# Two-layer transformer block on one core: second attention layer, weighted sums of the diagonal key tiles over all 512 queries

## The reference

```python
x = x + _L0_attn_ref(xn, ...) + _L0_ffn_ref(xn, ...)
xn = _layernorm(x, axis=-1)
x = x + _L1_attn_ref(xn, ...) + _L1_ffn_ref(xn, ...)
```

```python
scores = jnp.einsum('bhtd,bhsd->bhts', q, k)
mask = jnp.where(causal, 0.0, -jnp.inf)
probs = jax.nn.softmax((scores + mask) / jnp.sqrt(jnp.float32(dh)), axis=-1)
out = jnp.einsum('bhts,bhsd->bhtd', probs, v)
```

## Time and profile before

| | us |
|---|---|
| median of 3 runs | 2028.43 |
| lowest and highest of them | 2022.0, 2038.33 |
| the profiled execution | 2043.86 |
| its span, first to last instruction | 2042.1 |
| mean granted TensorE clock, share of full speed | 0.887 |

### The profile page before, as it was taken

The page is one execution under the profiler, slowest core; times in us unless marked ns, Lnnn a source line. Parts: engine busy times, 40 slices in busy tenths (PEclk is TensorE's granted clock), DMA queues, the critical chain, the costliest instruction groups (busy, mean ns, idle before and its releaser), DMA issues. The chain is left out here.

```text
span 2042.1 us, 35995 instructions
## 1 busy us (share of the span) xinstructions
PE 1633.4 (80%) x13931; PEld 819.6 (40%) x13931; DVE 1223.0 (60%) x2150; ACT 886.8 (43%) x1438; POOL 764.7 (37%) x423
## 2 busy tenths in 40 slices
PE   2468459879889898898989998345998889888887
PEld 2246325435354353544535443224654323333232
DVE  5323357686766757576576661481266877777761
ACT  0112215536456463564635455012322655555566
POOL 1500553564656656465564768260000111400000
PEclk9879759989899998999989999567998977888888
DMA  4113210000000000000000000123320000000000
GB/s 156 52 32 107 48 24 12 7 12 22 7 19 11 18 17 7 24 12 12 17 7 20 12 12 12 65 79 94 93 74 27 13 13 28 9 18 2 2 7 17
DMA packets 57109, 62.00 MB, mean 30 GB/s; under 512 B 12890, under 2 KB 42862, under 8 KB 56046
## 3 DMA queue, kind: packets, MB, share of 16 engines
q1 hardware_dynamic: 52846, 51.32, 8.1%
q0 software_dynamic: 4096, 8.40, 1.6%
HBM read 40.34 MB, written 18.48 MB: 29 GB/s over the span
## 5 line engine op out<-in xcount | busy, mean ns | idle before, releaser
L1582 POOL TENSOR_TENSOR a_prob_sum<-a_prob_sum,a_prob 128x1024 f32<-128x1024 f32 (+2 forms) x224 | 499.9, 2232 | 239.1 <-ACT a_prob L1530 218.2
L1530 ACT ACTIVATE a_prob<-a_st,a_table 128x512 f32<-128x512 f32 (+3 forms) x640 | 352.7, 626 | 358.3 <-PE a_st L1408 219.5
L1628 DVE TENSOR_REDUCE a_maxima<-a_ring 128x16 f32<-128x512 f32 (+3 forms) x640 | 352.8, 600 | 127.2 <-PE a_ring L1340 102.5
L1914 DVE TENSOR_REDUCE a_maxima<-a_mx 128x1 f32<-128x512 f32 (+3 forms) x640 | 352.3, 605 | 122.1 <-PE a_mx L1898 59.7
L2158 ACT ACTIVATE a_prob<-a_st 128x1024 f32<-128x1024 f32 (+3 forms) x320 | 269.0, 894 | 183.3 <-PE a_st L2076 102.4
L1435 PE MATMUL a_ot<-a_prob,a_values 128*64 128x512 f32 (+3 forms) x1280 | 289.0, 570 | 0.0
L1340 PE MATMUL a_ring<-a_k_hi,a_q_hi 64*128 64x512 f16 (+3 forms) x640 | 166.1, 373 | 94.2 <-DVE a_maxima L1628 71.6
L1898 PE MATMUL a_mx<-a_ks,a_qs 32*128 32x512 f16 (+3 forms) x640 | 188.3, 393 | 39.9 <-DVE a_maxima L1914 36.7
L2092 PE MATMUL a_ot<-a_prob,values_all 128*32 128x512 f32 (+3 forms) x1280 | 179.8, 638 | 0.2 <-ACT a_sums L2150 0.2
L2041 POOL DMA_INDIRECT a_back<-expert_out,slot_from x32 | 30.3, 948 | 347.7 <-ACT a_prob L2158 347.7
L1898 PEld LDWEIGHTS a_mx<-a_ks,a_qs 32*128 32x128 f16 x640 | 46.4, 93 | 246.8 <-DVE a_maxima L1914 173.8
(11 more groups left out here) (260 smaller groups left out, 2600.2 us busy)
## 6 DMA issues: line engine op xcount, KB each, us to landing
a_rden<-rden_wide SPq DMA_DIRECT2D x64, 128.0 KB, 2.9
f_w<-in_w SPq DMA_DIRECT2D x28, 256.0 KB, 2.8
expert_in<-zeros SPq DMA_DIRECT2D x5, 1024.0 KB, 11.2
f_rows<-expert_in SPq DMA_DIRECT2D x16, 256.0 KB, 3.7
expert_out<-f_result SPq DMA_DIRECT2D x16, 256.0 KB, 2.2
shared_w<-in_w SPq DMA_DIRECT2D x12, 256.0 KB, 3.1
a_table<-in_head_table SPq DMA_DIRECT2D x16, 140.5 KB, 2.2
parts<-part_t SPq DMA_DIRECT2D x4, 512.0 KB
```

The source lines that it names most:

```text
L1530: e = act.activation(prob[:, s % NPROB, a, c0:QW], ps_st[s % 2][:, a, c0:QW], ACT.Exp, bias=table[x][:, a, at:at + 1])
L1582: pool.tensor_tensor(into[:, :, c0:QW], into[:, :, c0:QW], here[:, :, c0:QW], ALU.add).then_inc(added, 2 if r == TPQ - 2 else 1)
L1628: dve.reduce_max(maxima[:, qt // TPQ, a, qt % TPQ, at:at + count], bank[:, 0:hi - lo].rearrange("p (w k) -> p w k", k=WINDOW), AX_X).then_ ...
L1914: dve.reduce_max(own.maxima[:, qt // TPQ, a, qt % TPQ, n:n + 1], bank[:, 0:hi - lo], AX_X).then_inc(done, 1)
```

## The change

For the diagonal tiles with r = 1, 2 and 3 there are now buffers of their own, one for each r: `prob_diag`, 128 by 3·4·512 float32. POOL fills them with zeros once, at the start of `attend1`. ACT writes the exponentials of the visible columns into them, always to the same columns, so that the columns left of 128·r stay zero. PE's weighted sum then runs over all 512 columns in every slot; on the hidden columns it adds zero times the values. `prob` stays for all other tiles, r = 0 among them. ACT waits for the zeros once, ahead of its first exponential. The exponentials, the scores, the masks, the maxima and all other waits are as before.

```diff
         prob = sb("prob", [P, 2, HPG1, QW])
+        prob_diag = sb("prob_diag", [P, TPQ - 1, HPG1, QW])
...
+        def prob_of(n):
+
+            qb, kt = SLOTS1[n % NS1]
+            r = kt - TPQ * qb
+            return prob_diag[:, r - 1, :, :] if r > 0 else prob[:, n % 2, :, :]
...
         @block.gpsimd
         def _(pool):
+            pool.memset(prob_diag[:, :, :, :], 0.0).then_inc(left_zero, 1)
...
             def weighted(m):
                 g, s = divmod(m, NS1)
-                (qb, kt), c0 = SLOTS1[s], first_col(s)
+                qb, kt = SLOTS1[s]
...
-                    mm = pe.matmul(ps_ot[32 * a:32 * a + 32, c0:QW], values_all[:, g, kt, a, :], prob[:, m % 2, a, c0:QW],
+                    mm = pe.matmul(ps_ot[32 * a:32 * a + 32, :], values_all[:, g, kt, a, :], prob_of(m)[:, a, :],
                                    start=kt == 0, stop=kt == TPQ * qb + TPQ - 1)
...
+            act.wait_ge(left_zero, 1)
             for n in range(ALL1):
...
-                    act.activation(prob[:, n % 2, 2 * half:2 * half + 2, c0:QW], ps_st[half][:, :, c0:QW], ACT.Exp,
+                    act.activation(prob_of(n)[:, 2 * half:2 * half + 2, c0:QW], ps_st[half][:, :, c0:QW], ACT.Exp,
                                    scale=SCALE1).then_inc(exp_done, 1)
```

More of the change, by code:

```diff
@@ L1982, in attend1 @@
         ring = own.ps_mx + [ctx.enter_context(nc.psum_tensor("a1_mx2", [P, QW], F32))]
+        left_zero = sem("left_zero")
         gathered = sem("gathered")
```

## The result

The changed kernel takes 2023.96 us, the median of 20 runs, against 2039.35 us for the kernel before in 20 runs. The ratio is 0.9929, with a 95% interval of 0.9909 to 0.9949: about 14.5 us faster, or 0.7%. The forecast was 31 us less, 1998 us, with a range up to 2020. The direction was right. The gain is half of the forecast, and the time lies outside the range.

The account below looks back on a forecast made before the run. In the second layer's attention, PE at a lowered clock was taken as the bound in places, DVE or ACT about as near at full clock. Clock −43.0, columns +12, fill 0 made −31 us: 2028.4 to about 1998, range 1984 to 2020.

Parts of the forecast that it names:

- The fill: Entry to the second layer's attention: POOL's zeros are ready 0.6 us before the first exponential, so cost 0 us.
- what the clock gives back: Second layer's attention: padded tiles look full to PE, so the clock falls should go, saving 43.0 us.
- What bounds the stage: Second layer's attention: PE sets the pace at the low clock; at full clock DVE or ACT is as near its limit.
- The rival of half the places: After narrow tiles: the clock holds in about half of the places, 2019 us; chance 0.12.
- the one that the clock does not answer: Narrow tiles: padding doesn't keep the clock up, leaving cost alone, 2034 to 2049 us, likeliest 2040; chance 0.12.
- the one that PE becomes the bound: Narrow stretches: the low clock lies over them too, so all added columns show, 2049 to 2069 us; chance 0.04.
- the third rival: Narrow tiles: clock doesn't answer to padding, perhaps because idle gaps are what counts; 2034 to 2049 us, chance 0.12.
- The columns: Narrow tiles of 16 blocks: 20.5 us of added PE work, partly hidden by DVE, costing 12 us between 6 and 20.5.
- The bound of 0 to 1 us: Entry to the stage: range for the first exponential's delay if ACT's table load follows the new wait; taken as 0.
- the table load behind the wait for the zeros: Entry to the stage: ACT's 1.28 us load coming after the new wait would make the first exponential 0.7 us late.
- From the trace to the median: Whole kernel: profiled execution lies 15.4 us above the runs' median, so the median goes from 2028.4 to about 1998 us.

Follow-up runs that it names:

- zeros_only: Kernel before plus only the separate buffers, the fill and ACT's wait, weighted sums still narrow: 2043.40 us, ratio 1.0022 to before.
- double: Changed kernel with the hidden columns summed twice in the narrow tiles, zeros both times: 2045.82 us, one run.
- pieces: Changed kernel with POOL's three long operations at the end of the gathers cut into 32 pieces: 2022.75 us, ratio 0.9896 to before.
- before_again: Kernel before, unchanged, run again for a second trace and more times: 2043.95 us over 12 runs.
- ones: Changed kernel with the hidden columns filled with ones in place of zeros: 2030.42 us, one run.
- late_fill: Changed kernel, POOL filling only hidden columns after DVE's first three a_neg_max, ACT waiting before its second tile: 2024.07 us over six runs, ratio 0.9898 to before.
- both: Changed kernel with the later, smaller fill and POOL's long operations in pieces together: 2016.98 us, ratio 0.9888 to before.

## Why the forecast was half right

Two terms of the sum failed. The fill was put at 0 us and cost 6.2, by a mechanism that the prediction didn't have; and what the clock gives back was put at 43.0 us, from one execution, where a usual one gives some 31. The terms one by one:

**What bounds the stage.** Right. Every full tile at the lowered clock in the earlier trace rows takes the time of the earlier trace rows once the clock is up, and at the full clock DVE, or ACT in the last group, is as near its limit as PE. The rival of half the places, the one that the clock does not answer and the one that PE becomes the bound all fall: `zeros_only` against the changed kernel has the clock from 0.86 to 0.98 and the loop from 449.5 to 428.0, with the columns as the only difference. Idle gaps of this size, which the third rival named, are not what counts here: in the stretch that answers to 6.94 us PE idled 0.69 us before, and the clock fell; in the changed kernel it idles 1.0 us (7.50 − 6.49 in the like stretch above), and the clock holds.

**The columns: 12 us forecast, 10.5 measured in the same trace, 9.2 against the other two with narrow sums**, and 0.6 in the tail. The 12 was a value near the middle of 6 and 20.5 and not worked out, so that it came near is in part luck; `double` shows that it was near the edge, behind which the full price is paid.

**The clock: 43.0 us forecast, 36.7 measured in the same trace** (344.9 us outside the narrow stretches before, 308.2 after), **some 31 in a usual execution** (21.6 net and 9.7 for the columns, by the means). The mechanism was right, and this term of the sum was too large by 12 us, the largest error in it. 6 of the missing 6.3 us are the one block with POOL's long multiply. This term had two errors. The one is that I counted the fall in group 1's block 3 as one like the others and did not look at what else could thin PE's work there; DVE's `a_neg_max` beside POOL's 7 us operation is in the trace of before. (Not all of the 6 us is its work: in `pieces`, without the stall, the fall came too and the full tiles still took 38.6 us, 3.7 over their like.) The other is larger in kind: the sum was made on one execution, which had 142 us at the lowered clock in the loop, where `before_again` had 111 and `zeros_only` 125. A saving that is made of clock falls has the spread of the falls, and the spread of before's runs was a sign of it: I carried that spread to the time, but not to the size of the saving.

**The fill: 0 us forecast, 6.2 measured.** This is the step whose mechanism failed. The prediction looked at who waits for the zeros (ACT, 0.6 us to spare) and not at who works beside the fill. The Trainium skill says it (SBUF — State Buffer, section "Who interferes with whom"): VectorE and GpSimd share one pair of SBUF ports, which is held for a whole instruction, and VectorE's scalar operations can take a mode that needs it. The traces agree: `a_neg_max` took 4.99 us beside the fill and 0.17 us without it, and in the changed kernel it was held to the end of POOL's instruction each time that it started beside one, while DVE's reduction of 16 columns started inside the fill and took its usual 0.18 us. The bound of 0 to 1 us was also too narrow for the part that I did name. The prediction feared the table load behind the wait for the zeros; it came behind the wait for the scores, which the second semaphore had made an instruction of its own, and so cost its whole 1.28 us however early the zeros were. 4.8 and 1.3 make the 6.2 us to within 0.1. No run has the one without the other.

**The sum, set right.** −21.6 in the loop, the columns' 9.7 in it, +6.2 at the entry, +0.6 in the tail: −15 us, by the mean of three traces with narrow sums.

**From the trace to the median.** The forecast went from a profiled execution to the median of three runs by subtracting 15.4 us. Over 20 runs before's median is 2039.35, so 11 of the 26 us by which 1998 misses 2023.96 are the base. The other 15 are, as near as can be told, the terms above: 12 of the clock, 6 of the fill, less 2 of the columns.

**What stays open.** Which of the first tiles of block 3 are followed by a fall differs between kernels that have the same instructions there: the changed kernel and `ones` have one fall in three traces alike, `late_fill` and `both` three, `pieces` four. The kernel before differs in its falls between its own executions. Most of those left come where PE waits for DVE in slots with an extra product in the ring, but not all: one comes at the start of the last group's block 3, where DVE has hardly any work, and one of `pieces` in a padded stretch (12.5 us in place of 8.9). So the padding makes falls rare and doesn't exclude them. What decides between one execution and another was not found.

## What to carry to other kernels

Columns of zeros in the matmuls of a thin stretch can pay for themselves where TensorE's clock falls behind that stretch and another engine sets the pace at the full clock: 20.5 us of matmul cost about 10 us and gave back some 31 in a usual execution. Here they had to stand in the thin stretch itself, and only up to the cover that the other engine gives, since the second helping cost its full price. Before a fill or any long GpSimd operation is costed at nothing, look for VectorE's scalar operations from SBUF to SBUF beside it (here these were held, and the reductions were not), above all those at the head of a stage's chain. A wait added ahead of ScalarE's first activation can move its table load onto the chain; and where a saving is made of clock falls, take it from several traces.

## What the hardware showed that I had not expected

- The clock fell from 2.4 to 1.2 GHz behind stretches in which PE was busy nine tenths of the time with short matmuls (6.25 of 6.94 us); PE's longest idle gap in that stretch was 0.2 us, and in any of the 16 it was 0.75 us.
- A fill of 5.22 us on POOL made a 0.17 us operation of DVE 4.99 us long, a multiply of 7.03 us made another 3.44 us long, and gathers of 0.94 us made others 0.36 to 0.41 us long. DVE's reductions and its copies out of PSUM beside the fill and the multiply kept their times.
- With a second semaphore to wait for, ACT's first exponential had its table load (1.28 us) behind the wait for its scores, at 1571.41 us, and not under it as before, at 1568.06 us.
- With the same kernel the loop took 454.2 and 445.3 us in two executions, while the padded one took 428.04 and 428.13.
